# Local attention's maxima taken off by VectorE instead of TensorE, in all batches, with a new order of steps

## The reference

```python
x = x + attn_a(layernorm(x))   # 16 heads of 8, rotary, causal over 256 positions ("front")
x = x + ffn(layernorm(x))      # silu(gate) * up, 352 wide, inputs quantised to FP4 in blocks of 16 ("ffn_a")
x = x + attn_b(layernorm(x))   # 16 heads of 8, windows of 32 positions ("local")
x = x + ffn(layernorm(x))      # the same weights again ("ffn_b")
```

```python
qkv = einsum('bglc,cd->bgld', x in groups of 32, w_qkv); q, k = rmsnorm(q, ln_w), rmsnorm(k, ln_w)
att = einsum('bghqd,bghkd->bghqk', q, k) / sqrt(8), masked causally within the 32
att = softmax(att); y = einsum('bghqk,bghkd->bghqd', att, v); return y @ w_proj
```

## Time and profile before

| | us |
|---|---|
| median of three runs | 405.03 (404.0 to 407.5) |
| the profiled execution | 405.48 |
| its span, first to last instruction | 403.7 |
| PE / PEld / DVE busy | 323.9 / 209.0 / 296.9 |
| ACT / POOL busy | 220.9 / 118.1 |
| mean granted TensorE clock | 0.918 |

### The profile page before, as it was taken

How to read it: one execution, slowest core, us unless ns; L and a number is a source line. 1 busy time by engine, 2 the same in 40 slices (tenths; PEclk the granted TensorE clock), 3 DMA queues, 4 the chain that set the end, 5 groups by cost and what they waited for, 6 DMA issues and landing times.

```text
span 403.7 us, 10370 instructions
## 1 busy us (share of the span) xinstructions
PE 323.9 (80%) x4197; PEld 209.0 (52%) x4197; DVE 296.9 (74%) x688; ACT 220.9 (55%) x610; POOL 118.1 (29%) x212
## 2 busy tenths in 40 slices
PE   3686866885988979799889987978999986778655
PEld 2343533472564548366656664655566554464433
DVE  2899093496368776987897878778988799856754
ACT  3215633734584485588648843884489445463211
POOL 1121150072036044414615350225052133140200
PEclk9998985995799999999999999999999999969565
DMA  6462424024005200500160025000000000000000
GB/s 188 142 148 79 80 80 78 2 68 90 2 2 126 36 2 18 141 2 5 40 133 2 2 74 99 2 2 15 2 2 2 15 2 13 3 1 15 2 13 13
DMA packets 33059, 17.53 MB, mean 43 GB/s; under 512 B 2100, under 2 KB 32756, under 8 KB 33012
## 3 DMA queue, kind: packets, MB, share of 16 engines
q1 hardware_dynamic: 33012, 16.87, 17.5%
HBM read 9.53 MB, written 7.34 MB: 42 GB/s over the span
## 4 chain that ended last, share of the span: by engine, by line
PE 47%; DVE 29%; ACT 9%; issue 4%; POOL 3%; ACTq 0%; DVEq 0%; POOLq 0%
DVE bmax L1467 8%; PE banks L979 8%; PE banks L730 5%; PE banks L992 4%; PE banks L869 4%; PE banks L763 3%; PE banks L853 2%; PE banks L938 2%; PE banks L787 2%; PE banks L898 2%; PE banks L857 2%; ACT prob L1105 2%; PE banks L987 2%; DVE nmaxl L1514 2%; PE banks L741 2%
## 5 line engine op out<-in xcount | busy, mean ns | idle before, releaser
L1105 ACT ACTIVATE prob<-banks 128x384 f32<-128x384 f32 x128 | 56.1, 488 | 12.8 <-PE banks L763 11.2
L1467 DVE TENSOR_REDUCE bmax<-banks 128x6 f32<-128x768 f32 x64 | 57.7, 950 | 4.5 <-PE banks L763 4.0
L763 PE MATMUL banks<-maskb,identb 64*128 64x128 bf16 (+1 forms) x512 | 45.1, 260 | 0.0
L763 PEld LDWEIGHTS banks<-maskb,identb 64*128 64x128 bf16 x512 | 26.5, 102 | 8.8 <-issue 4.1
L869 PE MATMUL banks<-prob,Vf 128*32 128x128 f32 (+1 forms) x512 | 28.1, 338 | 0.6 <-ACT oTf L1048 0.6
L1551 DVE SCALAR_TENSOR_TENSOR fa__hg<-fa__th,banks 128x352 f32<-128x352 f32 x16 | 8.3, 519 | 27.4 <-ACT fa__th L1189 27.3
L853 PE MATMUL banks<-Qf,Kf 48*128 48x256 bf16 x128 | 19.0, 294 | 8.4 <-ACT prob L1105 6.3
L979 PE MATMUL banks<-wguT,fa__xqT 128*128 128x352 f32 x56 | 22.8, 535 | 0.4 <-DVE fa__h L1552 0.4
L857 PE MATMUL banks<-nmTf,chooseb 64*128 64x384 bf16 x128 | 22.8, 352 | 0.0
L979 PE MATMUL banks<-wguT,fb__xqT 128*128 128x352 f32 x56 | 20.0, 479 | 2.3 <-DVE fb__h L1552 1.8
L938 PE MATMUL banks<-nmaxl,identf 128*128 128x512 f32 x32 | 16.9, 638 | 4.8 <-DVE nmaxl L1514 4.6
(11 more groups left out here) (246 smaller groups left out, 866.0 us busy)
## 6 DMA issues: line engine op xcount, KB each, us to landing
scr_f<-partsf SPq DMA_DIRECT2D x16, 192.0 KB, 2.5
Qf<-scr_f SPq DMA_DIRECT2D x16, 192.0 KB, 3.4
Kf<-scr_f SPq DMA_DIRECT2D x16, 192.0 KB, 4.5
scr_f<-partsf SPq DMA_DIRECT2D x16, 128.0 KB, 2.3
xall<-in_L_attn_a_x_dram SPq DMA_DIRECT2D x8, 128.0 KB, 3.2
scr_f<-partsf SPq DMA_DIRECT2D x16, 64.0 KB, 1.7
out_dram<-xall SPq DMA_DIRECT2D x8, 128.0 KB, 1.8
ropet<-in_rope_dram SPq DMA_DIRECT2D x1, 512.0 KB, 4.8
```

The costliest lines, as they stand in the source:

```text
L763: mm = pe.matmul(ends(S[j], cols), identb[rows, (half + j) % 2, :], maskb[rows, at:at + n].unsqueeze(1).to_broadcast([64, 2, n]), start=Fa ...
L1105: act.activation(prob[:, h % 8, :], bank[h % 3][:, 0:384], ACT.Exp).then_inc(f.s_exp, 1)
L1467: dve.tensor_reduce(bmax[:, 2 * g:2 * g + 2, :], banks[:, first:first + 2, 0:384].rearrange("p h (n k) -> p h n k", k=P), AX.X, ALU.max).t ...
```

## The change

`SHIFTED` names the batches in which DVE, right behind the reduction, adds the negated maxima to the scores in PSUM and writes the sum to `probl` in SBUF (a new step for each r). It is all eight. PE's product L938 goes in these batches, its `s_st_ps` signal comes from DVE's add, and ACT's Exp reads `probl` and writes it in place. The step of PE that held the products stays, empty. `TIMES` is new for all engines: `dve.local2` has two more positions in each row (reduction, add, reduction, add, normalise, residual) and most other positions move. Of `TIMES` only the rows that the text speaks of are shown; a row is a batch.

```diff
...
     "pe.front2": """
...
-290 291 293 295 296 299 301 302 307 310 313 316 318 321 323 326 328 331 332 336 338 341""",
+286 287 291 293 294 295 297 298 303 305 306 307 309 311 313 315 319 321 322 325 327 329""",
...
     "dve.front2": """
...
-82 83 86 87 93 94 95 96 97 110 113
-115 116 118 119 120 121 122 124 126 146 149
-154 155 157 159 160 162 163 165 167 186 189
-191 192 193 195 196 201 202 204 206 223 226
-228 229 230 232 233 235 237 238 240 262 264""",
+82 83 87 88 89 91 92 94 96 109 113
+117 118 120 121 122 123 125 126 128 144 148
+153 154 155 157 158 159 160 161 163 185 189
+194 195 196 198 199 200 201 202 204 223 227
+231 232 234 235 237 238 239 240 242 261 263""",
...
     "dve.local2": """
-85 89 99 102
-125 127 135 138
-156 158 168 175
-194 197 207 210
-234 236 243 251
-267 268 275 280
-299 300 306 308
-317 318 322 324""",
+85 90 93 95 100 104
+127 129 130 132 138 141
+164 166 167 169 174 179
+205 207 209 212 219 224
+244 246 248 250 260 264
+281 282 283 284 288 291
+310 312 313 315 320 322
+331 332 333 335 338 340""",
...
@@ -598,6 +598,8 @@
 
         LATE = (LAST - 1, LAST)
 
+        SHIFTED = range(NBATCH)
+
         def split_sum(engine, b):
             engine.tensor_tensor(qk[:, :, :], ra[:, :, :], rb[:, :, :], ALU.add).then_inc(qk_ready, 1)
 
@@ -933,7 +935,7 @@
                                                Kl[rows, w * P:(w + 1) * P], start=False, stop=True, skip_group_check=True)
                     mm.then_inc(l_half if c == 0 else l.s_sc_ps, 1)
                 yield
-                for r in range(2):
+                for r in range(0 if b in SHIFTED else 2):
                     pe.wait_ge(l.s_nmax, 2 * b + r + 1)
                     pe.matmul(bank[4 + r], identf[:, :], nmaxl[:, r, :, :].rearrange("p t g -> p (t g)").unsqueeze(2).to_broadcast([P, H, LS]),
                               start=False, stop=True, skip_group_check=True).then_inc(l.s_st_ps, 1)
@@ -1155,7 +1157,7 @@
                 for r in range(2):
                     yield
                     act.wait_ge(l.s_st_ps, 2 * b + r + 1)
-                    act.activation(probl[:, r, :], bank[4 + r], ACT.Exp).then_inc(l.s_exp, 1)
+                    act.activation(probl[:, r, :], probl[:, r, :] if b in SHIFTED else bank[4 + r], ACT.Exp).then_inc(l.s_exp, 1)
                 for r in range(2):
                     yield
                     act.wait_ge(l.s_probT_ps, 2 * b + r + 1)
@@ -1513,6 +1515,13 @@
                     dve.wait_ge(l.s_sc_ps, b + 1)
                     dve.tensor_reduce(nmaxl[:, r, :, :], bank[4 + r].rearrange("p (t g k) -> p t g k", t=T, k=LS), AX.X, ALU.max,
                                       negate=True).then_inc(l.s_nmax, 1)
+                    if b in SHIFTED:
+                        yield
+                        if b > 0:
+                            dve.wait_ge(l.s_probT, 2 * b)
+                        dve.wait_ge(l.s_nmax, 2 * b + r + 1)
+                        dve.tensor_tensor(probl[:, r, :].rearrange("p (g k) -> p g k", k=LS), bank[4 + r].rearrange("p (g k) -> p g k", k=LS),
+                                          nmaxl[:, r, :, :].rearrange("p t g -> p (t g)").unsqueeze(2).to_broadcast([P, H, LS]), ALU.add).then_inc(l.s_st_ps, 1)
                 yield
                 dve.wait_ge(l.s_o_ps, b + 1)
                 o = bank[4][:, 0:T * H * (HD + 1)].rearrange("p (t h e) -> p t h e", t=T, e=HD + 1)
```

More of the change, by code:

```diff
@@ L84 @@
 85 90 92
-129 135 137
-177 182 189
-228 234 239""",
+128 131 139
+173 177 183
+224 230 236""",
     "pe.front2": """
@@ L117 @@
 72 75 78 88 93 95 99
[L118 to L123, removed]
-    "pe.ffn_b2": """
[L125 to L130, removed]
+115 118 121 132 135 136 140
+170 175 181 214 217 219 222
+226 228 234 261 263 265 268
+275 277 280 314 317 318 320
+323 326 331 348 351 352 354
+355 357 358 365 369 374 376""",
+    "pe.ffn_b2": """
+141 144 154 185 188 189 191
+200 202 206 237 241 242 245
+252 254 257 285 289 290 292
+301 304 310 334 336 337 339
+340 342 345 359 362 363 366
+368 370 373 385 387 388 389
 391 392 395 403 404 405 406
@@ L135 @@
     "act.weights": """
[L136 removed]
+33""",
     "act.front1": """
 0 2 3 4 5 6
[L139 to L140 removed]
+7 8 10 13 18
+29 35 37 38 39
 41 67 71 72 74
 76 106 111 112 114
[L143 to L145 removed]
+116 148 158 159 161
+164 196 205 206 209
+211 247 259 260 263""",
     "act.front2": """
[2 rows of a table removed]
[2 rows of a table added]
 77 79 80 82 83 86 87 89 90 91 92 93 95 96 97 98 99 102 103 104 107 110
[4 rows of a table removed]
[L154 removed]
[4 rows of a table added]
+314 317 318 320 321 323 324 325 326 327 331 332 334 335 336 338 339 342 343 344 346 350""",
     "act.local1": """
 81 85 100 105 108
[L157 to L162, removed]
+117 151 155 157 163
+165 202 204 207 212
+252 255 256 258 265
+300 305 307 309 312
+348 354 356 357 361
+377 379 381 384 386
 397 398 400 403 405""",
     "act.local2": """
[L165 to L170, removed]
+118 119 120 121 131
+168 173 176 183 191
+217 220 221 225 238
+270 282 289 290 298
+322 328 333 345 351
+365 367 368 369 373
 391 392 393 394 396
@@ L175 @@
 75 78
[L176 to L181, removed]
+115 123
+180 187
+228 239
+261 293
+319 329
+353""",
     "act.ffn_a2": """
-46 49 57 66 70 73
+46 49 57 65 70 73
 84 88 94 101 109 113
[L185 to L190, removed]
-    "act.ffn_b1": """
[L192 to L197, removed]
+127 132 138 147 152 156
+195 199 203 215 233 241
+249 253 257 268 278 284
+299 302 303 315 337 341
+347 349 352 362 370 372
+374 375 376 385 390""",
+    "act.ffn_b1": """
+150 153
+198 200
+246 251
+306 310
+355 359
+378 382
 399 402
@@ L200 @@
     "act.ffn_b2": """
[L201 to L206, removed]
+160 162 166 188 208 210
+213 214 222 250 262 264
+266 267 273 294 308 311
+313 316 330 340 358 360
+363 364 366 371 380 383
+387 388 389 395 401 404
 406 407 408 413 416 417
@@ L214 @@
 20 27 28 30
-31 40 42 44
-45 56 58 59
-60 71 73 74""",
+31 39 42 43
+44 54 56 57
+58 69 72 73""",
     "pool.front2": """
@@ L222 @@
 26
[L223 to L226, removed]
+36
+50
+64
+79""",
     "pool.local1": """
 21 24
[L229 to L233, removed]
+32 40
+45 55
+65 70
+76 82
+89 94
 98 102
@@ L239 @@
 29 33 34
-43 47 48
-57 61 62
-72 75 76
-85 86 87
-95 96""",
+46 47 48
+60 61 62
+71 75 77
+84 86 87
+90 92""",
     "pool.ffn_a2": """
@@ L247 @@
 25
-36
-55
-70
-84
-94
+37
+59
+74
+85
+96
 101""",
     "pool.ffn_b1": """
-35 37 38
-50 51 52
-65 66 67
-77 79 80
-90 91 92
+35 38 41
+51 52 53
+63 66 67
+80 81 83
+91 93 95
 99 100 103
@@ L264 @@
 49
-64
-82
-89
+68
+78
+88
 97
@@ L314 @@
 56 68 69 70
-81 90 91 92
-114 129 130 131
-152 164 170 173
-190 198 200 203
-227 241 245 247
-265 269 271 273 276""",
+81 97 98 99
+134 136 137 139
+171 176 177 178
+191 214 216 220
+245 251 252 253
+265 268 275 277 278""",
     "dve.ffn_a2": """
@@ L323 @@
 71 72 73 74 75 84
-98 100 101 103 105 109
-137 142 144 145 147 172
-178 181 183 184 185 213
-218 219 220 221 224 248
-253 257 258 259 261 277
-281 283 284 286 288 290 293 295 296 297 302""",
-    "dve.ffn_b1": """
-104 106 107 108
-139 140 141 143
-177 179 180 182
-212 215 216 217
-252 254 255 256
-282 285 287 291
-309 310 311 312
-325 326 327 328 329""",
-    "dve.ffn_b2": """
-128 132 133 134 136 153
-161 166 169 171 176 199
-205 208 209 211 222 231
-239 242 244 246 250 263
-266 270 272 274 278 289
-298 301 303 305 307 314
-316 319 320 321 323 330
-331 332 333 334 335 336 337 338 339 340 341""",
+101 102 103 105 107 115
+146 150 152 165 170 181
+188 192 193 206 210 217
+222 226 229 243 247 258
+262 267 270 274 279 290
+294 295 296 298 300 302 305 307 309 311 317""",
+    "dve.ffn_b1": """
+106 108 110 112
+142 143 145 147
+180 183 184 186
+225 228 230 233
+266 269 271 273
+293 297 299 301
+323 324 325 326
+341 342 343 344 345""",
+    "dve.ffn_b2": """
+124 131 133 135 140 162
+168 172 173 175 187 203
+208 211 213 215 221 241
+249 254 255 256 257 276
+280 285 286 287 289 304
+308 314 316 318 321 328
+330 334 336 337 339 346
+347 348 349 350 351 352 353 354 355 356 357""",
 }
```

40 lines of the change are left out of this document (20 added, 20 removed), and 36 rows, old and new, of the table TIMES.

## The result

The changed kernel takes **421.78 us** (median of 4 runs, 417.68 to 424.17) against 405.09 for the kernel before in the same sitting: a ratio of 1.035, 95% interval 1.029 to 1.041. A run more than 1.5% above the fastest of its kernel is left out of every ratio, here the one of 424.17 (the two medians as they stand would give 1.041). The forecast was 401.8, the range 396.5 to 408.5. The profiled execution took 420.81 us, its span is 419.0.

What follows compares the result with a forecast made beforehand. The prediction took PE and DVE to bound the kernel in turn. Stage terms -1.0, -4.1 and +1.9 sum to -3.2 us: 402.3 for a run like the profiled one, 401.8 as median, range 396.5 to 408.5.

Steps and rivals of the forecast that it cites:

- Stage 1: 125 to 160 us, one batch of local attention: 1.70 us leaves the chain, half of 1.44 comes back, -1.0 us.
- stage 2: 160 to 315 us, four batches: busier engine falls 3.7 us; at the same 89.5% fill 150.9 us replaces 155, -4.1.
- stage 3: 315 us to the end, three batches: +1.4, 0, then -0.3 and +0.9 us, taken as +1.9.
- The signs of being wrong: Adds over 0.8 us, front's end moving under 4 us, tail over 5 longer, or a lower clock in a middle slice.
- The prices of the instructions: At the changed lines: adds of 0.69 us on DVE, Exp 0.63 us; DVE busy 308 us.
- The adds' share in stage 2: 160 to 315 us: of 5.8 us of adds, what falls into DVE's 25.7 us of idle is free.
- full-price rival: DVE bounds everywhere: 9.34 us of products leave the chain, 11.5 of adds enter, 407.2 us; chance 0.07.
- The rival of the backlog: Behind front2's last step: 11 moved DVE steps and six adds, 13.4 us more, lengthen the tail; 406 to 411, chance 0.12.
- Exp's 0.1: Exp reading SBUF instead of PSUM, last batches: between nothing and 0.2 us at the end, taken as 0.1.
- The clock rival: TensorE, with 17 us less work, gets one more low-clock stretch, about +4 us; 405 to 406; chance 0.16 shared with no effect.

Runs made afterwards that it cites:

- Experiment 6: Kernel before without the 16 products and without adds (maxima taken, not subtracted; Exp reads PSUM): 411.55 us, ratio 1.015.
- Experiment 7: Kernel before with neither maxima, products nor adds in local attention, Exp of the bare scores: 407.89 us, ratio 1.006.
- Experiment 11: Kernel before without products or adds, plus spare bf16 products on PE in the two gaps where its clock fell: 407.76 us, ratio 1.004.
- experiment 5: Kernel before plus a spare 128x512 SBUF add on DVE behind each local reduction, for which nobody waits: 417.7 us, ratio 1.030.
- experiment 1: Changed kernel put back to the old order, each add in its reduction's step, no products: 422.62 us, ratio 1.041 to the kernel before.
- experiment 2: Changed kernel's new order with the products kept and no adds: 417.76 us, ratio 1.028 to the kernel before.
- experiment 4: Kernel before, old order, with adds in batches 6 and 7 only and products in the other six: 408.28 us, ratio 1.005.
- experiment 9: Kernel before with spare bf16 products on PE in batches 1 and 2 and, in all batches, ahead of turning the front's maxima: 407.21 us, ratio 1.006.
- 10: Old order without products or adds, plus spare bf16 products in batches 1 and 2 and ahead of every turning of maxima: 409.74 us, ratio 1.010.
- 3: Changed kernel with a spare 512-column f32 product on PE behind each add, before the wait for Exp: 424.93 us, ratio 1.046 to the kernel before.
- 8: New order with neither products nor adds, maxima taken but not subtracted: 424.6, 423.77, 423.57 and 416.45 us, too far apart for a ratio.
- experiment 12: Changed kernel with spare bf16 products on PE at two of its own clock falls: 422.84 us, ratio 1.041 to the kernel before.

## Why the prediction was wrong

Between the forecast sum of -3.2 us and the measured +15.3 of the profiled executions lie 18.5 us: 6.7 ahead of the front's end (stages 1 and 2, -5.1 forecast, +1.6 measured) and 11.8 behind it (stage 3, +1.9 forecast, +13.7 measured). The signs of being wrong that the prediction named came, but for the adds' price: the front's end later, the tail longer by more than 5 us, the lower clock in the middle.

**The prices of the instructions were right.** Add 0.69 forecast, 0.682 measured; Exp 0.63 and 0.629; DVE busy 308 and 307.8. That the broadcast operand costs nothing is shown (it is 16 values read 32 times each, and not the reverse as the text has it).

**The step that failed ahead of the front's end is stage 2, "The busier engine falls by 3.7 us. Filled to the same 89.5%, the stretch is 135.1/0.895 = 150.9 us".** It turned busy time taken from PE into time. Experiment 6 did just that taking, with nothing put in, and the kernel got slower by 1.5%. Experiment 7 took DVE's reductions as well and gained nothing. The fill is no constant: with less to do PE waits for the same chains, and behind those waits its clock falls (0.59 at 130 to 140 us), which puts part of the work back (316.9 us busy for the expected 307). Experiment 11 bears it out in part, since spare work in two gaps gave 3.8 of 6.1 us back. PE's busy time forecast at 307 was 324.3.

**The adds' share in stage 2** ("what falls into DVE's 25.7 us of idle is free") held, if anywhere, in the new order. In the old one 11.3 us of spare DVE work cost 12.2 us (experiment 5), and sixteen adds put where nothing stood cost 11.1 (from experiment 6 to 1; 10.7 with each sitting's own kernel before taken off), for 10.9 us of adds. So in the old order the adds have their full price, and the 9.3 us of products that the full-price rival took off did not come off. In the new order, from experiment 2 to the change, the adds for the products cost 4.0 us, and the intervals of the two ratios overlap.

**The step that failed behind it, and the larger one, is stage 3: the sum has nothing for the new order's later start of local attention. The rival costed the order by its number of steps; what mattered was where local attention of one batch ends.** The rival of the backlog had the size: 13.4 us more DVE work behind the front forecast, 14.1 measured (77.83 less 63.75), and a tail 13.7 us longer. Its condition, that it decides from a front's end of 302 us on, was met by far: 316.6. It had a chance of 0.12, since I took its steps for ffn work that nobody waits for at once. By the positions nine of the eleven are ffn steps, but four of these are batch 4's ffn_b, which needs batch 4's local residual, and that residual is a tenth. In experiment 2, without an add, DVE has 10.7 us more behind the front and the tail is 14.0 longer. In all nine kernels with the old order (before, 1, 4 to 7, 9 to 11) batch 4's local residual is 16.5 us ahead of the front's last and the tail 88 to 93 us; in all five with the new one (the change, 2, 3, 8, 12) it is 0.4 behind and the tail 102 to 106. The positions in the diff said so beforehand. On DVE the local residual of batch 4 stands at 251 in the old order, 13 steps ahead of the front's last at 264; in the new one at 264, right behind 263. Then three batches remain to be finished, at 25 us each, where part of the first had been done. DVE's mean load in the tail (72%), which the text let speak against the rival, says nothing of such a chain.

**Stage 3, +1.9 us,** was for the arithmetic alone, and low for that too: batches 6 and 7 had +0.6 and cost 2.6 in the tail (experiment 4), all three +1.9 and 4.6 (experiment 1). Its terms with Exp's 0.1 make 2.1, not the 1.9 that was taken. It left out the lag, which is the greater part.

**Stage 1, -1.0 us:** the front's residual of batch 3 moved from 158.7 to 159.5 us, local attention's of batch 0 from 143.2 to 149.7. The clock at 130 to 140 us went from 0.86 to 0.51. The saving did not come.

**The clock rival** had the mechanism and put it at 4 us, "one more such stretch". There are three in the middle: 0.51 at 130 to 140, 0.56 and 0.76 at 200 to 220, 0.66 at 290 to 300 us. The argument against it, that 160 to 315 us stood at 1.00, was a state of the kernel before and no property of the stretch.

**What stays open.** How much of the changed kernel's time ahead of the front's end is the clock and how much is waiting: experiment 12 moved the falls and not the end. Where the clock falls depends on gaps that move with it, so one such trial can't price the whole. Whether the new order without products and adds is better than with the products is open, with runs from 416.45 to 424.6. Why the adds cost 16.8 us in the old order and 4 in the new one is not shown: where DVE's reductions stand differs, and so does much else. The lag and the longer tail go together in all fourteen kernels; an order that differs in the lag alone was not tried, so that the lag by itself makes the tail longer rests on the reckoning of 16.9 less 3.1.

## What to carry to other kernels

Before costing an edit to a pipelined kernel in written order, find in the positions where the last stage of each batch stands against the end of the stage that sets the pace: here the time after that end was three batches of 25 to 26 us and the last ffn's 26.5, less the 16.5 us by which local attention was ahead before and is no more. A lag of 17 us was worth 14. Busy time taken from an engine is worth nothing until a kernel with only that removed shows it; such a kernel (experiment 6 or 7 here) is the first to run, since it bounds the whole idea. For PE it can even cost, as it did here, where the remaining work ran in part at the lower clock.

## What the runs showed of the hardware

Taking 16.9 us of f32 products away lowered TensorE's mean granted clock (medians of the runs 0.903 and 0.887) and made the run 1.5% longer; 4.0 us of spare products in two gaps brought 0.59 back to 1.00 in one stretch and the run back to 1.004. More clock was not more speed everywhere: from 30 to 125 us a rise from 0.84 to 0.95 brought the front's residuals 0.8 us forward at most (experiment 9), and in the changed kernel two falls filled were followed by others and the time stayed (experiment 12). A VectorE add with one operand broadcast by a stride of zero (16 values, 32 times each) and the other in PSUM took 682 ns for 128x512, against 687 for the plain PSUM times SBUF operation of that size, and the one between SBUF operands alone 709. VectorE time put in behind the local reductions was paid 1.08 for 1 (experiment 5), and 8.8 us of it taken out together with the products gained nothing (experiment 7). The Trainium skill (page "Perfetto Trace Analysis", Identifying the Most-Contended Engine) would have TensorE judged by MFU and by the share of its weight loads, and the engine with the highest occupancy optimized first. By the loads' 52% against 74% that was VectorE in the kernel before: experiment 5 agrees with it, experiment 7 does not. MFU was not worked out here.
